# Vision tower layer on one core: unread products in TensorE's pauses, one product per global maximum, first down integers on two engines

## The reference, cut to what is computed

```python
# tokens: patches (b, 49, 768), RMS norm, 8-bit integers per row, times a ternary weight
xq   = act_quant(rms_norm(patches))
h    = concat([cls, einsum('bnd,od->bno', xq, weight_quant(weight))], 1) + pos
# attention: three passes over layernorm(h), 16 heads of 16, causal, each with its own weights
for i in range(3):
    q, k, v = heads(xp @ Wq[i].T + bq[i]), ...
    w   = softmax(causal(q @ k.T * 4))
    out[i] = layer_norm((w @ v) @ Wo[i].T + bo[i], ln_g[i], ln_b[i])
h    = h + layer_norm(concat(out) @ Wout.T + bout, ln2_g, ln2_b)
# feed forward with 8-bit steps that come from a maximum over the whole tensor
def act_fake_quant(x, clip):
    scale = sigmoid(clip) * max(abs(x)) / 127          # one number for all 64 x 50 tokens
    return clip(round(x / scale), -128, 127) * scale
xq   = act_fake_quant(layernorm(h), clip_x)
hh   = silu(xq @ q8(w_gate).T) * (xq @ q8(w_up).T)      # 704 wide
h    = h + act_fake_quant(hh, clip_down) @ q8(w_down).T
```

## Time and profile before

| | |
|---|---|
| three runs | 770.28, 771.28, 774.87 us; median 771.28 |
| the profiled execution | 769.84 us, its span (first to last instruction) 768.1 us |
| mean granted clock of PE | 0.975 of 2.4 GHz |
| busy in the span | PE 684.5 us (89%), DVE 641.9 (84%), ACT 584.3 (76%), POOL 520.0 (68%) |
| first block, second block | up to about 674 us, from there to 768.1 |

### The profile page before, as it was taken

One profiled execution on the slowest core, in us unless ns is written; L12 is line 12 of the kernel. 1 busy time (PEld: TensorE's weight loads), 2 busy tenths in 40 slices (PEclk: granted clock), 3 DMA queues, 4 the chain that ended last, 5 costly groups with the idle time before them and its releaser, 6 DMA issues. The chain is left out here.

```text
span 768.1 us, 25770 instructions
## 1 busy us (share of the span) xinstructions
PE 684.5 (89%) x9862; PEld 535.2 (70%) x9862; DVE 641.9 (84%) x1395; ACT 584.3 (76%) x1280; POOL 520.0 (68%) x793
## 2 busy tenths in 40 slices
PE   0498799999999999999999999999999999568866
PEld 0277678777877787877877787788778777334455
DVE  4788876899889988989898899889987898759947
ACT  3567888687788678869778878688868887379875
POOL 3459965957687859877677789478948786521154
PEclk9979999999999999999999999999999999869979
DMA  8301000000000000101000000100100000000005
GB/s 240 100 28 33 17 19 17 19 18 20 4 32 27 10 2 34 34 2 33 18 19 3 16 19 3 34 18 18 41 3 22 20 22 22 1 1 1 0 24 148
DMA packets 14980, 21.95 MB, mean 29 GB/s; under 512 B 1992, under 2 KB 11466, under 8 KB 14860
## 3 DMA queue, kind: packets, MB, share of 16 engines
q1 hardware_dynamic: 14424, 19.91, 8.4%
q10 hardware_dynamic: 436, 0.40, 0.4%
HBM read 17.03 MB, written 3.28 MB: 26 GB/s over the span
## 5 line engine op out<-in xcount | busy, mean ns | idle before, releaser
L905 POOL TENSOR_TENSOR k_bd<-kT,rmask 128x400 f32<-128x400 f32 x192 | 167.8, 902 | 7.5 <-PE ps_s L1358 4.3
L806 ACT COPY pT<-ps_w 25x400 f32<-25x400 f32 x192 | 94.8, 494 | 9.2 <-PE ps_w L1373 6.7
L1399 PE MATMUL ps_w<-oy_hi,o_hi 128*128 128x512 f32 x192 | 94.9, 494 | 0.0
L914 POOL TENSOR_TENSOR prob_hi<-prob_hi,rsum 128x800 f32<-128x800 f32 x48 | 74.9, 1559 | 13.3 <-DVE rsum L1151 13.3
L1134 DVE TENSOR_REDUCE nmax<-ps_s 128x16 f32<-128x400 f32 x96 | 72.4, 765 | 11.6 <-PE ps_s L1358 11.3
L786 ACT COPY v_bd<-ps_w 50x256 f32<-50x256 f32 x192 | 70.4, 367 | 13.2 <-PE ps_w L1333 10.9
L1399 PE MATMUL ps_w<-oy_hi,o_lo 128*128 128x512 f32 x192 | 76.3, 397 | 0.0
L1399 PE MATMUL ps_w<-oy_lo,o_hi 128*128 128x512 f32 x192 | 76.2, 397 | 0.0
L827 ACT ACTIVATE ps_w<-ps_w 128x256 f32<-128x256 f32 x96 | 35.6, 371 | 51.7 <-PE ps_w L1399 50.3
L1358 PE MATMUL ps_s<-k_bd,qT 64*25 64x200 f32 (+1 forms) x3072 | 70.5, 291 | 0.0
L919 POOL TENSOR_TENSOR ln<-ln,ln_eps 128x1 f32<-128x1 f32 x96 | 19.9, 208 | 74.6 <-ACT ps_w L827 74.1
(11 more groups left out here) (237 smaller groups left out, 2070.4 us busy)
## 6 DMA issues: line engine op xcount, KB each, us to landing
x_in<-in_x SPq DMA_DIRECT2D x64, 147.0 KB
out<-hidden SPq DMA_DIRECT2D x14, 200.0 KB
pT<-in_tok_w SPq DMA_DIRECT2D x1, 768.0 KB, 6.5
hidden<-in_wq SPq DMA_DIRECT2D x1, 768.0 KB, 8.6
k_bd<-in_wk SPq DMA_DIRECT2D x1, 768.0 KB, 9.5
v_bd<-in_wv SPq DMA_DIRECT2D x1, 768.0 KB, 9.2
hidden<-in_wout SPq DMA_DIRECT2D x1, 768.0 KB, 9.3
hidden<-in_wo SPq DMA_DIRECT2D x1, 768.0 KB, 10.8
```

The costliest lines, as they stand in the source:

```text
L806: last = nc.scalar.copy(pT[ROWB * h:ROWB * h + LQ, s % 2, c::2, :, 0:LQ], ps_w[row:row + LQ, bank].rearrange("p (j t) -> p j t", j=4)[:, : ...
L905: last = nc.gpsimd.tensor_tensor(k_bd[:, v % KBD, c], kT[:, w % 2, c, 2 * p * L:(2 * p + 2) * L].unsqueeze(1).broadcast_to([P, HR, 2 * L]) ...
L914: nc.gpsimd.tensor_tensor(pr, pr, rsum[:, s % 2, e].unsqueeze(2).broadcast_to([P, H, WIDTH[e]]), ALU.mult).then_inc(prob_ready, 1)
L1399: mm = nc.tensor.matmul(G[:], ot[:, s % 2, c, 2 * (p % 2):2 * (p % 2) + 2].rearrange("p b t -> p (b t)"), wt[:, w, c], start=False, stop=( ...
```

## The change

Four things are done.

1. Unread products. `keep_busy(n)` issues n products of 128 x 512 in bf16 whose result nobody reads: 18 behind the step "beta" of the opening and 32 behind PE's last step of the first block (both into bank 0 of `ps_s`), 9 behind the first search for the maximum, and 10 ahead of and 10 behind the second (into bank 1 of `ps_w`). The ten ahead of the second search wait for ACT's last silu. The others wait for nothing of their own.
2. The maximum by one product. In place of transpose, reduction on one partition and spreading product, one fp32 product with the column of maxima broadcast to 128 x 128 and the identity puts all 128 maxima in each partition's row; DVE reduces on all partitions into `mx` and goes on from there. `one_f`, `top` and a memset of POOL are gone.
3. The first down integers. Of groups 0 and 1, ACT makes the slices (1, 2, 4, 5) and (0, 1, 2, 3), DVE the slices (0, 3) and (4, 5). DVE also casts the first half of group 0 (L1672 of the changed kernel), which POOL did; PE's first products wait for that (`first_h`). ACT's wait from group 2 on is for one cast fewer than before.
4. `PER_GROUP` has an entry "kbd" for which `AT` has no step.

```diff
@@ first block, PE
+            def keep_busy(products):
+                for _ in range(products):
+                    nc.tensor.matmul(ps_s[:, 0, 0], id16[:], tokT[:, 0:2].rearrange("p c n -> p (c n)"), start=True, stop=True)
...
                     for k in range(NS * KC):
                         mm = nc.tensor.matmul(G[0:1, 0:D], bcol[:, k:k + 1], st_out[:, k], start=(k == 0), stop=(k == NS * KC - 1))
                     filled_by(mm, step)
+                    keep_busy(18)
...
             walk("pe", do)
+            keep_busy(32)
@@ second block, ACT
-                    act.wait_ge(hq_ready, 2 * (g - 1) + 2 * T)
-                    for f in range(FC):
+                    if g > 1:
+                        act.wait_ge(first_h, 1)
+                        act.wait_ge(hq_ready, 2 * (g - 1) - 1 + 2 * T)
+                    for f in ((1, 2, 4, 5), (0, 1, 2, 3))[g] if g < 2 else range(FC):
@@ POOL
-            nc.gpsimd.memset(one_f[:], 1.0).then_inc(f_zeroed, 1)
...
-                for a in (0, 1):
+                for a in (1,) if g == 0 else (0, 1):
                     fs = slice(FP * a, FP * a + FP)
-                    pool.wait_ge(hint_ready, g * FC + FP * (a + 1))
+                    pool.wait_ge(hint_ready, 4 if g == 0 else 7 + a if g == 1 else (g - 1) * FC + 2 + FP * (a + 1))
+                    if g < 2 and a == 1:
+                        pool.wait_ge(hint_v_ready, (2, 4)[g])
@@ DVE (the same for the second maximum, with mx[:, 3:4])
-            dve.wait_ge(max_turned, 1)
-            nc.vector.tensor_reduce(top[:, 0:1], ps_s[0:1, 0, 0, 0:P], AX.X, ALU.max).then_inc(max_found, 1)
-            dve.wait_ge(all_max, 1)
-            nc.vector.tensor_scalar(sg[:, 0, 0:1], ps_s[:, 0, 1, 0:1], clip_sig[:, 0:1], 1.0 / QMAX, ALU.mult, ALU.mult).then_inc(step_chain, 1)
+            dve.wait_ge(max_spread, 1)
+            nc.vector.tensor_reduce(mx[:, 1:2], ps_s[:, 0, 0, 0:P], AX.X, ALU.max).then_inc(max_found, 1)
+            dve.wait_ge(max_found, 1)
+            nc.vector.tensor_scalar(sg[:, 0, 0:1], mx[:, 1:2], clip_sig[:, 0:1], 1.0 / QMAX, ALU.mult, ALU.mult).then_inc(step_chain, 1)
...
+            def h_ints(g, fs):
+                for f in fs:
+                    nc.vector.tensor_scalar(h_int[:, g, f], acts[:, f, g * GT:(g + 1) * GT], hcol[:, 2, f:f + 1], None,
+                                            ALU.mult).then_inc(hint_v_ready, 1)
+            h_ints(0, (0, 3))
+            dve.wait_ge(hint_v_ready, 1)
+            dve.wait_ge(hint_ready, 2)
+            dve.wait_ge(f_zeroed, 3)
+            nc.vector.tensor_copy(h_q[:, 0, 0:FP, :, 0:L], h_int[:, 0, 0:FP].rearrange("p f (n t) -> p f n t", n=GB)).then_inc(first_h, 1)
+            h_ints(1, (4, 5))
@@ PE
-                nc.tensor.transpose(ps_s[0:1, 0, 0, 0:P], mx[:, 2 * n:2 * n + 1], id32[:]).then_inc(max_turned, 1)
-                pe.wait_ge(max_found, n + 1)
-                nc.tensor.matmul(ps_s[:, 0, 1, 0:1], one_f[:], top[:, n:n + 1], start=True, stop=True).then_inc(all_max, 1)
+                nc.tensor.matmul(ps_s[:, 0, 0, 0:P], mx[:, 2 * n:2 * n + 1].broadcast_to([P, P]), id32[:],
+                                 start=True, stop=True).then_inc(max_spread, 1)
...
+            def keep_busy(products):
+                for _ in range(products):
+                    nc.tensor.matmul(ps_w[:, 1], id16[:], wgT[:, 0, 0:2].rearrange("p f k t -> p (f k t)"), start=True, stop=True)
             find_max(0)
+            keep_busy(9)
...
             turn_wd(1, 0)
+            pe.wait_ge(silu_ready, GROUPS * FC + 3)
+            keep_busy(10)
             find_max(1)
+            keep_busy(10)
...
-                        pe.wait_ge(hq_ready, 2 * g + a + 1 + 2 * T)
+                        if g == 0 and a == 0:
+                            pe.wait_ge(first_h, 1)
+                        else:
+                            pe.wait_ge(hq_ready, 2 * g + a + 2 * T)
```

22 lines of the change are left out of this document (11 added, 11 removed).

## The result

| | before | changed |
|---|---|---|
| median, us | 770.78 (6 runs, 768.67 to 774.87) | 764.5 (6 runs, 762.84 to 766.25) |
| ratio changed / before | | 0.9914, 95% interval 0.9885 to 0.9944 |
| profiled execution, us | 769.84, span 768.1 | 765.96, span 764.2 |
| mean granted clock | 0.975 | 0.985 |

The six runs of the changed kernel had clocks between 0.983 and 0.992, and their times follow them: 766.25 at 0.983, 762.84 at 0.992. The profiled one, at 0.985, is the second longest of them, 1.5 above their median; the profiled one of before is 0.9 under its own. So the two profiles differ by 3.9 us of span, the medians by 6.3.

A forecast was written before the change was run, and what follows sets the result against it. PE sets the pace in attention, leaving pauses at the opening and two searches; ACT's integers bound the down projection. 1.0 + 2.15 + 0.47 + 2.05, about 5.7 us, from 769.84 gives 764.2, adjusted to 764.9; range 761.2 to 769.5.

The forecast's parts named there:

- Price 0.215 us at the high clock: Cost claimed for one unread product of 512 columns on PE; 0.41 us at the low clock.
- The slower rival: Unread products in the opening and ending block 1 run at the low clock and delay PE: 775.3 us, chance 0.04.
- Opening, 1.0 us: 18 products keep the clock high into the embedding; gain 1.0 us, bounds -0.9 to +1.45.
- the first paragraph of the prediction: PE paces attention from 96 to 653 us, so time won before 50 us arrives at its end almost whole.
- First maximum, 2.15 us: Search and first gate and up products of block 2 gain 2.15 us, bounds 0.25 and 2.7.
- both of its terms: At the first maximum: 0.64 us from 0.26 of shorter chain and faster transposes, 1.5 from faster first products.
- A fall in a pause all the same, chance 0.19: Rival: clock falls in a remaining hole, at the first search, the down projection or both; 766.8 us, chance 0.19.
- The argument against it: Against a fall in a pause: three earlier falls came 4 to 5.2 us after the last work, longer than remaining holes.
- Second search, 0.47 us: One spreading product removes a DVE wait and second PE trip at the second maximum; gain 0.47 us, between 0.3 and 0.6.
- Down projection, 2.05 us: ACT makes 44 integer rows, not 48, with a quicker PE start; gain 2.05 us, bounds 0.2 and 2.1.
- The step that failed: Down projection: relieving ACT alone wins some 0.2 us, as the PE and DVE loop, delayed by its slow first group, follows closely.
- I added 0.7: Half of the 1.4 us by which before's median exceeded its profiled execution, raising 764.2 to 764.9.

The follow-up runs named there:

- r4: Changed kernel with the two-step search of before at both maxima, POOL's memset of `one_f` back; 765.45 us, ratio 0.9919.
- r0: Changed kernel again, no edit, for a second profile; 765.84 us, ratio 0.9924.
- r11: Kernel before again, no edit, for a second profile; 771.17 us, ratio to before 1.0004.
- r9: r8 with five more unread products before an embedding and five before a head projection of the early groups; 760.41 us, ratio 0.9853.
- r1: Changed kernel without the 18 unread products of the opening; 767.15 us, ratio 0.9948.
- r2: Changed kernel without the 32 products ending the first block and the 9 behind the first search; 766.35 us, ratio 0.9936.
- r6: Changed kernel without the split, ACT making all 48 integer rows and POOL all casts; 767.04 us, ratio 0.9951.
- r10: Changed kernel with 128 bf16 transposes in place of the 32 unread products at the end of the first block; 766.11 us, ratio 0.9912.
- r3: Changed kernel without the ten and ten unread products around the second search; 764.04 us, ratio 0.9915.
- r8: Changed kernel with more unread products: 5 and 3 in the opening, 8 late in attention, 38 instead of 32 ending block 1; 760.6 us, ratio 0.9865.
- r5: Kernel before with only the split of the first down integers, no unread products, old search; 770.65 us, ratio 0.9981.
- r12: r9 with 14 instead of 9 products behind the first search, 3 behind the integers' first turn, 4 behind an opening turn; 759.74 us, ratio 0.9866.

## Why the prediction was right, and where it was not

The forecast was 764.9 with 761.2 to 769.5; the median was 764.5. By its own steps:

**Unread products.** Price 0.215 us at the high clock: 0.22 measured. The 18 end at 35.73 and not 34.9, since they start later, and PE still has 0.85 us to spare. The 32 end at 673.41 and PE waits another 1.94 us for the change of block. Hidden, as said. The slower rival (fillers at the low clock) did not come true; r4 shows its mechanism for nine of them: begun 0.36 later and 0.30 slower, they hold up the transposes by 0.66 us.

**Opening, 1.0 us.** 1.40 came to 49 us in this profile, 0.64 in r0 (against before's profile), 1.3 in the mean of seven profiles against four, and what stayed to the end of block 1 cannot be read from one profile. What this profile does not bear out is the first paragraph of the prediction, that time won before 50 us arrives at the end of attention almost whole. The middle has falls of its own, in some executions and not in others, and they are as large as the gain: between the key products' start and the last 64 small products changed took 609.35 us, and before 608.15 in one profile and 609.71 in the other (r11). So 1.20 went there in this pair; that it is the falls at 69 and 92 is argued, since profiles without a fall in that stretch took 605.3 (r9) to 608.15 us. A further 0.88 went at the end of attention (7.71 against 6.83 us), where the clock was low for 6.8 us and not 3.4. 1.40 - 1.20 - 0.88 + 0.02 = -0.66. By the medians of r0 and r1 the opening is worth 1.3 us, within an uncertainty as large. So for the median the sentence on the middle is neither shown nor refuted.

**First maximum, 2.15 us.** 2.17 measured, and both of its terms hold: ACT lets little of the shorter chain through (its integers begin 3.23 us into the stage and not 3.58; where the clock stays low 0.15 us of it is left, r2; 0.26 was forecast), and the high clock at the transposes and the first products gives the rest (2.02 by r2; 0.38 and 1.5 forecast). The place of the limit was right too: with the old search in r4 ACT's integers start at the same 3.23 us. The nine products were to end a microsecond ahead of PE's transposes; at the low clock they ended just as these began.

**A fall in a pause all the same, chance 0.19.** It happened at this place in changed, r0, r4, r6 and r10, and not in r1, r3 and r8, which have the same 9 products there. The argument against it, that the falls came 4 to 5.2 us behind the last work and no hole left is as long, does not hold: at 676.2 the clock fell 2.8 us behind the last unread product, with four records of small fp32 products in between. It cost 0.1 us here (the stage takes 11.16 to 11.23 us with this fall and 11.09 to 11.10 without), because the nine products stood behind it and had it up again before the first gate product. So the rival's event was right and its price wrong, by the luck of where the fall lies; r9, with the same nine, paid 1.1 us.

**Second search, 0.47 us.** 0.42. The fp32 product takes 0.49 for two records, 0.45 was chosen. r4 adds that only 0.21 belongs to the product: the wait of 0.67 that I took as one "whose clock was still high at its start" is 0.47 where the clock stays high, so 0.20 of it came from the fall at 732.5.

**Down projection, 2.05 us.** 1.98, for a reason that was half wrong. ACT's rows (44 in 22.96), the 9.07 behind them and the hand-over at 2.2 us (2.3 forecast) are as worked out. Single prices were high: two DVE rows 0.77 and not 1.2, the cast 0.79 and not 1.0. But 0.47 of waiting between them was missing: DVE needs ACT's second row too, and that ends at 733.31. Two later rows took 1.72. The step that failed is "taking work from ACT alone would win some 0.2 us; it needs a faster start as well", if the start is meant as the clock. The split brings its own faster start: DVE hands over the first half 0.9 us sooner. In r5 PE's first group took 1.0 less besides, since the clock rose before its end; in r3 it took 4.97 at the low clock, and the start of 0.9 was enough. r5 and r3 show 32.09 and 32.25 us with a low clock, 32.07 with a high one. The ten and ten products are thus worth 0.0 to 0.2 us here and 0.2 in the search at most (and that only if the fall comes in the search; in r3 it came behind it).

**Transposes.** The sum did not rest on it, but the text leaned on the rule of the Trainium skill (TensorE: Matmul & The Clock Gate, Part 4: PE-mode transpose) that a transpose doesn't count as work in the same way. r10 speaks against it where the clock is already high: 7.3 us of transposes alone held it at 1.00. Whether transposes can raise it was not tried.

**Median against profile.** I added 0.7 for the place of before's profile among its runs. The changed kernel's own profile then lay 1.5 above its median. That is as large as any term of the sum, and the median's agreement to 0.4 us is in part chance.

What stays open: what decides in which execution the clock falls at 69, 94 or 544 us. The traces do show what stood ahead of it. At 69 it fell in the two profiles in which PE had a hole of 2.2 us there (changed and r6); in the twelve others no hole at that place was longer than 1.4. At 544 the hole was 2.27 us, up to 542.11 (r5). Near 94 all the falls (changed, r0, r3, r6, r8, r5, r11) came 0.3 to 2.2 us behind holes of 1.2 to 1.9 us, but before and r1 had a hole of 1.8 and no fall. Nor is all of r12's early end of block 1 explained by falls: r1 and r4 have none between the key products and block 2 and take 621.6 us for that way, r12 takes 619.8, r9 619.5.

## What to carry to other kernels

Where an engine's clock follows its work, unread products in a pause are free if they end before the engine is next needed, and are worth what the next stage loses at the low clock, if the engine is the late one there: in this kernel 2.0 us at one place, about nothing at another. Count them at the low clock before placing them, because a fall may already have come. When a bound is a loop of two engines close behind a third, price the edit's effect on the loop's start too before saying that it needs help; and when one stretch of the kernel changes from execution to execution, read stages between fixed instructions, and repeat the unchanged kernel before reading a difference of 2 us in it.

## What the runs showed of the hardware that was not expected

- The clock also falls in the middle of attention, at 69, 94 and once at 544 us, where PE is busy for nine tenths of a slice, behind holes of 1.2 to 2.3 us in its work; before has it too (r11). With five products more at each of two of these places, r9 and r12 had no such fall. Held up throughout, the kernel's runs (five) agree within 0.35 us, where they differed by 5 to 8 before: most of the spread of this kernel went with the clock.
- A fall can come 2.8 us behind the last large product (changed, 676.2).
- Transposes alone held the high clock for 7.3 us (r10).
- Ahead of the first recorded event the granted clock may not be what it says: in before the stretch from 22 to 29 us reads 1.00, while six products of 256 columns take 1.44 to 1.46 us there, as they do at 0.50, and 0.83 at the high level in the changed kernel (38.35 us).
- DVE makes an int8 row of 400 from fp32 in 0.385 us and casts 1,200 int8 elements to bf16 in 0.79. Two such rows during which POOL made a cast (734.41 to 735.59) took 1.72 us; that the cast is the reason was not tried.
